# An attention quad's weighted sums: one pair in each of four slots, or two pairs at the end of slots 1 and 3

## The reference

```python
qkv = h @ qkv_w + qkv_b                                # h: the norm of x, cut into shifted windows
q, k, v = split(qkv)                                   # per window and head
attn = einsum('wqhd,wkhd->whqk', q * scale, k)         # scores
attn = softmax(attn + rel_bias + mask)
o = einsum('whqk,wkhd->wqhd', attn, v)                 # weighted sums
x = x + (o @ proj_w + proj_b)
x = x + mlp(norm(x))
```

## Time and profile before

| | |
|---|---|
| median of 3 runs | 8522.53 us (8521.94 to 8527.99) |
| the profiled execution: its time | 8519.52 us |
| its span (first to last instruction) | 8517.4 us |
| busy: PE, PEld | 7998.7 us (94%), 5982.3 us (70%) |
| busy: DVE, ACT, POOL | 6092.7 us (72%), 5147.7 us (60%), 5399.7 us (63%) |
| the chain of work that ended last | PE 71%, DVE 10%, issue 9%, ACT 3% |
| mean granted TensorE clock | 0.995 of full speed |
| DMA | 142.14 MB, mean 17 GB/s |

### The profile page before, as it was taken

One profiled execution on the slowest core, in us unless ns is written; L12 is line 12 of the kernel. 1 busy time (PEld: TensorE's weight loads), 2 busy tenths in 40 slices (PEclk: granted clock), 3 DMA queues, 4 the chain that ended last, 5 costly groups with the idle time before them and its releaser, 6 DMA issues.

```text
span 8517.4 us, 316110 instructions
## 1 busy us (share of the span) xinstructions
PE 7998.7 (94%) x111420; PEld 5982.3 (70%) x111420; DVE 6092.7 (72%) x18216; ACT 5147.7 (60%) x9120; POOL 5399.7 (63%) x6723
## 2 busy tenths in 40 slices
PE   3999999999999999999999999999999999999997
PEld 1777777777777777777767777777776677777766
DVE  4777767767776776776777677776686767777666
ACT  1755747646674664755767476574576647567456
POOL 6865646556785665655778465564677756556566
PEclk9999999999999999999999999999999999999998
DMA  2100010000011011000001101000100110000001
GB/s 42 22 13 10 15 27 15 10 12 13 10 21 31 13 20 22 15 6 16 9 15 21 27 16 27 15 15 4 20 4 19 24 22 15 7 13 14 6 19 23
DMA packets 596906, 142.14 MB, mean 17 GB/s; under 512 B 595660, under 2 KB 596256, under 8 KB 596471
## 3 DMA queue, kind: packets, MB, share of 16 engines
q1 hardware_dynamic: 574102, 131.41, 7.8%
q10 hardware_dynamic: 16865, 3.97, 0.3%
q0 software_dynamic: 5504, 1.21, 0.1%
HBM read 31.68 MB, written 19.27 MB: 6 GB/s over the span
## 4 chain that ended last, share of the span: by engine, by line
PE 71%; DVE 10%; issue 9%; ACT 3%; DVEq 2%; POOL 2%; ACTq 1%; POOLq 0%; DMA 0%
PE ps L876 12%; PE ps L932 11%; PE ps L838 8%; PE ps L864 7%; PE ps L948 7%; PE ps L977 7%; PE ps L883 5%; PE ps L901 4%; PE ps L911 3%; ACT PT L743 3%; DVE bst L995 2%; PE ps L819 2%; PE ps L920 2%; DVE xn L1114 2%; PE ps L962 2%
## 5 line engine op out<-in xcount | busy, mean ns | idle before, releaser
L618 POOL TENSOR_TENSOR S<-S,mx 113x588 f32<-113x588 f32 (+1 forms) x2048 | 2065.4, 1009 | 1543.8 <-DVE mx L1156 1539.4
L743 ACT ACTIVATE PT<-ps 98x588 f32<-98x588 f32 (+1 forms) x2048 | 1182.5, 577 | 1218.6 <-PE ps L932 1211.3
L1154 DVE TENSOR_TENSOR S<-ps,bias 113x588 f32<-113x588 f32 (+1 forms) x1536 | 963.4, 627 | 863.7 <-PE ps L864 863.7
L876 PEld LDWEIGHTS ps<-Vbd,PT 98*49 98x49 f32 x40960 | 1107.5, 125 | 658.6 <-issue 634.7
L876 PE MATMUL ps<-Vbd,PT 98*49 98x18 f32 (+1 forms) x40960 | 1321.4, 201 | 165.8 <-ACT PT L743 125.9
L1156 DVE TENSOR_REDUCE mx<-S 113x12 f32<-113x588 f32 (+1 forms) x2048 | 1359.6, 664 | 70.6
L932 PEld LDWEIGHTS ps<-ident,S 113*98 113x98 f32 x10240 | 1033.9, 128 | 477.6 <-issue 388.9
L932 PE MATMUL ps<-ident,S 113*98 113x113 f32 x10240 | 1338.7, 261 | 7.8 <-ACT S L725 4.6
L725 ACT ACTIVATE S<-S 113x588 f32<-113x588 f32 (+1 forms) x2048 | 1239.9, 605 | 63.1 <-POOL S L618 61.3
L948 PEld LDWEIGHTS ps<-w,G 128*98 128x98 f32 x12288 | 1149.8, 167 | 160.2 <-issue 86.3
L948 PE MATMUL ps<-w,G 128*98 128x96 f32 (+1 forms) x12288 | 1151.5, 250 | 2.7 <-DVE x L1221 2.4
(11 more groups left out here) (104 smaller groups left out, 10891.0 us busy)
## 6 DMA issues: line engine op xcount, KB each, us to landing
Vbd<-Vd SPq DMA_DIRECT2D x1536, 41.3 KB
Vbd<-Vd SPq DMA_DIRECT2D x512, 38.3 KB
mask<-L_conv_mask_matrix_dram SPq DMA_DIRECT2D x256, 37.5 KB
x<-x_dram SPq DMA_DIRECT2D x48, 84.0 KB
out_dram<-x SPq DMA_DIRECT2D x48, 84.0 KB
x<-x_dram SPq DMA_DIRECT2D x228, 10.5 KB
out_dram<-x SPq DMA_DIRECT2D x228, 10.5 KB
out_dram<-x SPq DMA_DIRECT2D x180, 18.4 KB
```

Of the source, the lines that this page charges most:

```text
L618: pool.tensor_tensor(v, v, m, ALU.subtract).then_inc(a_sub, 1)
L743: act.activation(PT[:, (s + 3) % 4, 0:blocks, :, :].rearrange("p (b t) w n -> p b (t w) n", b=banks), PTps[:, PT_BANK[l] - 3:PT_BANK[l] - ...
L876: last = pe.matmul(Ops[ROW2 * w:ROW2 * w + N, p, b, :].rearrange("p (a n) -> p a n", a=2), PT[:, p, b, w, :], v, start=True, stop=True)
L1154: dve.tensor_tensor(dst, scores, b, ALU.add).then_inc(a_bi, 1)
```

## The change

The weighted sums leave their place behind the scores in all four slots. They now stand in slots 1 and 3 only, two pairs together, at the end of the slot, in front of the turning of the pair before (and behind the neighbouring quads' work). Slot 1 takes pairs 2 and 3 of quad i-1 and raises `a_pv`; slot 3 takes pairs 0 and 1 of quad i. No instruction is added or removed; all other engines' code is the same.

```diff
                                 last.then_inc(a_sc, 1)
-                            if on(-1) if s < 3 else on(0):
-                                wait(a_pte, i.pair(s - 3))
-                                p = (s + 1) % 4
-                                if s == 3:
-                                    wait(a_o, i - 1)
-                                    spread = (g * LAYER_QUADS + l * NQ + i.index - t + 2) * 32
-                                    pe.wait_ge(s_vb[t], spread if i.static else pe.snap(spread))
-                                for b in range(blocks):
-                                    for w in range(2):
-                                        v = values_of(Vbd[:, o if s < 3 else t, p, w, :, :], nh, b)
-                                        last = pe.matmul(Ops[ROW2 * w:ROW2 * w + N, p, b, :].rearrange("p (a n) -> p a n", a=2),
-                                                         PT[:, p, b, w, :], v, start=True, stop=True)
-                                if s == 2:
-                                    last.then_inc(a_pv, 1)
                             if s == 0 and on(-2):
...
                                 last.then_inc(a_t1, 1)
+                            if s in (1, 3) and (on(-1) if s == 1 else on(0)):
+                                if s == 3:
+                                    wait(a_o, i - 1)
+                                    spread = (g * LAYER_QUADS + l * NQ + i.index - t + 2) * 32
+                                    pe.wait_ge(s_vb[t], spread if i.static else pe.snap(spread))
+                                for p in (s - 3, s - 2):
+                                    wait(a_pte, i.pair(p))
+                                    at = p % QUAD
+                                    for b in range(blocks):
+                                        for w in range(2):
+                                            v = values_of(Vbd[:, t if s == 3 else o, at, w, :, :], nh, b)
+                                            last = pe.matmul(Ops[ROW2 * w:ROW2 * w + N, at, b, :].rearrange("p (a n) -> p a n", a=2),
+                                                             PT[:, at, b, w, :], v, start=True, stop=True)
+                                if s == 1:
+                                    last.then_inc(a_pv, 1)
                             if on(-1) if s == 0 else on(0):
                                 wait(a_pte, before)
```

## The result

| | before | after |
|---|---|---|
| median | 8522.53 us | 9873.55 us (5 runs, 9815.10 to 10251.95) |
| the profiled execution: time, span | 8519.52, 8517.4 us | 9941.70, 9939.5 us |
| mean granted TensorE clock | 0.995 | 0.884 (0.852 to 0.901 in the five runs) |
| busy: PE, DVE | 7998.7, 6092.7 us | 9106.0, 6118.4 us |

A forecast was written before the change was run, and what follows sets the result against it. TensorE bounds the kernel, meeting VectorE once a quad in slot 3. Quad terms +1.35 (layer 0), +1.30 (1, 2), +0.53 (3) sum to 574 us, counted as 538; on 8519.5 that makes 9057.5, plus 3.0: 9060 us, range 8920 to 9220.

The forecast's parts named there:

- The walk: One quad of layer 1 followed slot by slot, new minus before: +1.30 us a quad in layers 1 and 2.
- main term: Slot 3, before the turning of `Ot`: TensorE waits 1.29 us for VectorE's copy into `Vd`, no longer hidden by sums.
- the part for the exponential: Part of the 1.29 us wait perhaps falls a slot earlier, for pair 1's exponential, leaving the sum unchanged.
- The small terms: Layer 1: new waits 0.22 (`hT`) and 0.19 (`xn`), a covered wait of 0.07, each pair's sums at 0.66 us.
- The new waits for `hT` and `xn`: Keys in slot 0 wait 0.22 us for `hT`; turning in slot 3 waits 0.19 for `xn`; sums hid both before.
- 30 of 32 quads: First and last quads of each of 16 stretches, having gaps filled with other work, left out: 574 us became 538.
- The clock: Rival: gaps in each quad lose TensorE's full clock; one quad in four losing 2.12 us adds 254: 9314; chance 8%.
- the earlier trace: Trace rows before the change: after a 1.63 us gap six matmuls took 4.29 us instead of 2.17, 1.2 GHz for 2.4.
- The half: Rival: `hT` and `xn` in time, joined pairs 0.28 cheaper; +0.6 us a quad over 480 quads, 8811; chance 7%.
- the faster rivals: Rival: slot 3's wait goes because `a_pv` is raised in slot 1; all 165.8 us saved, 8357; chance 3%.
- TensorE's busy share: Predicted sign in the profile after: TensorE's busy share falls to about 88%.

The follow-up runs named there:

- the first filled one: Changed kernel plus one unread matmul of 512 columns in slot 3's gap, ahead of the turning of `Ot`, in all layers: 9189.58 us, ratio 1.078 to the kernel before.

## Why the prediction was right in direction and wrong in size

- *The walk* held in its main term. The new gap shows as 1.01, and 3294.16 - 3293.13 = 1.03 a slot earlier, where the values of i+1 stepped 0.77 before, is the part for the exponential: 0.26 more, 1.27 together for 1.29 forecast. The row of before:

```profile
3034.76 0.93 PE L901 MATMUL ps<-wqkv,hT 97*98 97x96 f32 x8
3035.53 0.74 PE L932 MATMUL ps<-ident,S 113*98 113x113 f32 x6
```

- *The small terms* were partly wrong, and that each stretch of a quad of layer 1 still came within 0.03 us (the table above), layer 0 at +1.42 for +1.35, layer 3 at +0.45 for +0.53, is in part luck: errors cancelled. The new waits for `hT` and `xn` were forecast at 0.22 and 0.19. The profile shows no idle time for them in the loop; the steps ahead of them grew by 0.12 (3299.85 to 3300.74, 0.89 for 0.77) and 0.09 (3296.43 to 3296.95, 0.52 for 0.43), and by the rows below TensorE goes on 0.05 after `hT` and `xn` are ready, not the 0.15 taken over from the exponential:

```profile
3300.02 0.67 ACT L748 ACTIVATE hT<-ps,gb 96x392 f32<-96x392 f32 x1
```

```profile
3296.07 0.83 POOL L640 TENSOR_TENSOR xn<-xn,rstd 98x384 f32<-98x384 f32 x1
```

A pair beside another takes 3298.64 - 3297.43 = 1.21 / 2 = 0.605, not 0.66. Against this, entering the sums from other work costs time that the sum did not have: the turning of `xn` now steps 0.48, before 0.34; the queries step 0.83, where 0.74 was forecast; and in the run with single pairs at the slots' ends the keys step 0.83 in front of the sums, where before they stepped 0.66 in front of the turning.

- *30 of 32 quads.* The quads' differences make 128 x 1.42 + 256 x 1.28 + 128 x 0.45 = 567 us for all 32; the run with the filler in layers 0 to 2 gives about 580. So the edges pay too, and the discount was wrong by some 40 us.
- *The clock* is the step that failed, as a term and as a chance. I gave 254 us at 8%: 2.12 us in one quad of four, with the argument that the new gap of 1.29 is shorter than the 1.63 of the earlier trace rows and partly split. Measured: 180 of 400 quads touched, not a quarter, and 790 / (180 x 512 / 400) = 3.4 us for each, 790 to 830 us in all. Even the pure gap of 0.95 (in the original order) was enough. The reasoning compared one gap with one gap, and the length of one gap does not settle it: in the run with single pairs at the end the gap of the earlier trace rows stands at the same place and the six matmuls behind it keep the full clock (2.24 us).

```profile
2323.60 2.24 PE L977 MATMUL ps<-h,w 97*128 97x392 f32 x6 [1.63 <-ACT G L783]
```

What the reasoning left out is that the new gap returns in every quad, and that a fall does not end with one short stretch: a settled quad of 17.07 us loses 4.30, every time, and in layer 3 a single fall cost all the quads that were left. The earlier trace rows had shown that a gap of this order can do it; I looked for no row in which such a gap returns and the clock holds. The sign that the prediction gave for this rival, a clock below full within the attention, came true.

- *The half and the faster rivals* had no part. TensorE's busy share, forecast to fall to 88%, stayed at 92%: a matmul at the lower clock counts as busy. Of the 1422 us that the profiled execution lost, TensorE's idle time holds only 1422 - 1107 = 315, so an idle-time view alone would have missed more than three quarters.

**Shown:** the gap filled keeps the clock (two kernels, two orders); the gap made in the original order loses it; pairing is not needed for it. **Open:** which mixture of idle time and work makes the clock fall, and what brings it back. A filler far from the gap mostly holds it. The single pairs at the slots' ends hold it in all counted quads of layers 0 to 2 (gaps of 0.5 to 0.6) and lose it in 98 of 100 in layer 3, with a gap of 0.8 to 0.9 ahead of the fall; with the filler in slot 0 layer 3 has the same gap of 0.90 and holds in 98 of 100. The changed kernel holds layer 3 in three groups and loses it in the fourth, though they run the same instructions. Since the changed kernel was not measured again beside the fillers, a part of the small differences in clock could also be another chip's; that the filler keeps the clock does not hang on this, as two unfilled kernels lost it beside the first filled one. The spread of the changed kernel's runs, 9815 to 10252, goes with their clocks, 0.901 down to 0.852; what decides in which quads a run loses it was not found.

## What to carry to other kernels

When a kernel is bound by TensorE, walk through one period on each engine between the places where they meet: here such a walk was good to 0.1 us a quad. But price any new idle time of TensorE that returns in every period twice, once as time and once as clock, and take for the second the whole stretch at half clock as the bad end; if it cannot be removed, a matmul that nobody reads, placed exactly inside the gap, is worth trying first. It repairs only the clock: the best filled run of the new order, 9130.61, is still 604 us behind the old one. A wait that needs a computed number is better issued before the semaphore that comes late than behind it. The order of the other waits around a late one counts as well, by 0.05 us here.

## What the runs showed of the hardware that was not expected

- A gap of 0.95 to 1.05 us in each quad of 12 to 13 us brought the clock from 2.4 to 1.2 GHz in up to two thirds of a layer's quads. The low state can sustain itself: settled quads of 17.07 us (layer 2), 13.0, 12.89 and 14.15 (layer 3, three kernels); in two of these, 12.89 and 13.0, TensorE has hardly any idle time left (0.0 and 0.06 us a quad) and the clock stays at 1.2 GHz all the same, for 355 and 331 us.
- One gap of 1.63 us at the same place was followed by the lower clock in one kernel and by the full one in another.
- More work made the kernel faster: 992 matmuls more on the page (two for each filler), 684 us less.
- The place of the filler matters by what waits there: inside the gap it costs 0.02 us a quad of layer 1, behind the keys 0.86.
- A computed wait behind a late semaphore cost TensorE 0.15 us once a quad in layer 1, 44 us or 0.5% of this kernel; TensorE went on 0.30, 0.15 and 0.10 us after the late division in three orders of the same three waits.
